# Late phase of a graph and mixture-of-experts kernel: 13 routing rounds with plans of their own, expert results added onto the output by DMA

## The chip, the cores and the metric

The kernel runs on 1 core of one Trainium2 chip. The metric is the device time of one execution in microseconds (us); lower is better. A core has a matrix engine (TensorE, PE in the profile), a vector engine (VectorE, DVE), a scalar engine (ScalarE, ACT), GpSimd (POOL) and SyncE (SP). The engines run their own programs in order and wait for each other by semaphores. SP, ACT and POOL issue DMAs; POOL issues the indirect ones, whose row numbers lie in a tile.

## The reference

Data is float32. 12,500 nodes with 256 features pass through a graph attention layer and a mixer block, whose sum with the input is x. The last layer, the one that this change is about, is a mixture of 8 experts in which each node uses its best two:

```
x = x + gnn(xn) + mix(xn)
xf = layernorm(x)
logits = xf @ gate_w + gate_b                   # 8 experts
probs = softmax(logits)
top2_vals, top2_idx = top_k(probs, 2)
cw = zeros(N, 8).at[arange(N)[:, None], top2_idx].add(top2_vals)
for each expert e:
    h = gelu(xf @ W1[e] + b1[e])                # 256 -> 512
    y = h @ W2[e] + b2[e]                       # 512 -> 256
    acc = acc + cw[:, e] * y
out = x + acc
```

## The kernel before

Four stages with barriers between them make the graph layer and the mixer; they end about 2,500 us into the program and the change does not touch them. After the last barrier comes the late phase, which has three kinds of work. A tile of nodes is 128 nodes (98 of them); a super is 4 node tiles (25 of them).

**Routing** takes a super from `xm_d` (mixer result) and `frag` (graph result, gathered by POOL into `e_fr`), adds them (`e_x`), stores the sum to `x1_d`, normalises it (`e_hn`, on DVE), transposes it on PE, multiplies by the gate and finds, in a chain of small DVE operations over a pair of supers, each node's two experts, their weights and its rows in a list for each expert. POOL then scatters each node's normalised features twice into `sorted_d`, once for each expert. The nodes are cut in two `PARTS` (56 and 42 node tiles). Only when a part is routed in full does `plan_vector` work out which expert tile holds which rows.

**Expert tiles** have 256 rows of one expert: 63 in the first part and 49 in the second, 112 in all, because each expert's last tile of a part is padded. W1 and W2 of all experts lie in SBUF. For each tile j there is `start` (PE turns the tile over, ACT copies it, DVE copies the expert's W1 to `w1c` and works out where results go and with what weight), `first` (16 matmuls with W1, ACT applies gelu), `second` (16 matmuls with W2) and `store` (DVE adds the bias and multiplies by the weight; POOL scatters the rows to `result_d`). `fetch` is SP's load of the tile into `gin`.

**Combining** reads the two results of each node and x1, adds them on DVE and stores `out`, super by super.

The order on every engine is written by generators that yield at the same steps: `back_half` routes part 0 alone, then runs the 63 tiles of part 0 with the routing of part 1 between them, three route steps at each yield, then the 49 tiles of part 1 with the combining of part 0 between them, then combines part 1. Within this, `tile_order` puts the pieces in this order on every engine: first(j), start(j+1), fetch(j+2), second(j-1), store(j-1). The fetch of before waits for these alone:

```
        if j >= 2:
            sp.wait_ge(S.x_tp, j - 1)
            sp.wait_ge(S.x_aim, j - 1)
```

`x_tp` counts tiles turned over on PE, `x_aim` tiles whose destinations DVE has worked out, `x_f1` halves of fc1 done, `x_h` gelus, `x_f2` tiles whose second is done, and `x_st` the two DVE operations of `store` (2 for each tile).

## Time and profile before

| | |
|---|---|
| time, median of 3 runs | 3830.7 us (3829.39 to 3833.43) |
| the profiled execution's own time | 3831.84 us |
| its span, first to last instruction | 3830.6 us |
| mean granted clock of TensorE | 0.863 of full speed |
| late phase | 2,500 us to the end |

The span is what the instructions cover; the profiled execution took 1.24 us more than that. The late phase is 1,331 us of it, and only there do the two kernels differ. Times in the rows further on are counted from the start of the span.

### The profile page before, as it was taken

The page shows a single profiled execution, that of the slowest core. Times are in us where ns is not written, and L with a number is a line of the kernel's source. Part 1 is how long each engine was busy: PE and PEld are TensorE (multiplying, and loading weights), DVE is VectorE, ACT ScalarE, POOL GpSimd, SP SyncE. Part 2 cuts the span into 40 slices and gives each one's busy share as a digit, 9 for nine tenths or more (in the row PEclk, how much of TensorE's full clock was granted, in tenths as well). Part 3 has the DMA queues.
Part 4 walks back from the last instruction along what each step waited for, and adds up shares of the span by engine and source line. Part 5 has one row for each costly group of instructions (what it writes and reads, how often), then busy time and mean ns, then how long its engine had stood idle before and what let it go on. Part 6 is the DMA issues. An engine that isn't in the chain of part 4 may idle for free.

```text
span 3830.6 us, 43808 instructions
## 1 busy us (share of the span) xinstructions
PE 2905.6 (76%) x12222; PEld 2286.9 (60%) x12222; DVE 2282.7 (60%) x6122; ACT 1380.5 (36%) x3103; POOL 2203.9 (58%) x2244
## 2 busy tenths in 40 slices
PE   6966878877777778887777764545398899989990
PEld 5844655555555555565555553345387778878880
DVE  6526666667666676666766665567565655445542
ACT  2313545444544444544544543100022222222220
POOL 0047777777777777777777776157535534323330
PEclk9977989898899998998999987555588889999995
DMA  8865665566555665656555655176433323255427
GB/s 210 275 185 153 182 162 158 160 169 169 162 159 155 165 176 157 163 163 179 157 162 162 166 148 131 50 243 197 145 115 120 111 82 117 73 177 182 149 70 235
DMA packets 412379, 602.91 MB, mean 157 GB/s; under 512 B 64458, under 2 KB 323694, under 8 KB 411935
## 3 DMA queue, kind: packets, MB, share of 16 engines
q0 software_dynamic: 106608, 306.41, 27.8%
q1 hardware_dynamic: 232563, 220.56, 19.0%
q10 hardware_dynamic: 72892, 72.50, 7.6%
q8 instruction: 104, 1.70, 0.2%
q14 instruction: 212, 1.74, 0.1%
HBM read 400.40 MB, written 198.88 MB: 156 GB/s over the span
## 4 chain that ended last, share of the span: by engine, by line
PE 51%; DMA 13%; POOL 12%; DVE 11%; issue 7%; ACT 4%; SPq 1%; ACTq 0%; DVEq 0%; POOLq 0%
PE bank L953 14%; PE bank L1732 9%; PE bank L1720 8%; DMA rows<-table,srcix 6%; PE bank L808 6%; POOL sorted_d L1330 5%; POOL rows L890 4%; PE bank L800 4%; DMA m_xs<-in_x 3%; DVE rows L1086 2%; PE bank L520 2%; DMA out<-c_x 2%; PE bank L512 1%; PE bank L513 1%; POOL e_fr L1313 1%
## 5 line engine op out<-in xcount | busy, mean ns | idle before, releaser
L890 POOL DMA_INDIRECT rows<-table,srcix x1664 | 1609.2, 967 | 506.9 <-issue 364.6
L953 PE MATMUL bank<-rows,onehot 128*128 128x272 f32 x3328 | 937.3, 431 | 30.4 <-ACT fout L1003 26.2
L1003 ACT ACTIVATE fout<-bank 128x272 f32<-128x272 f32 x1664 | 640.6, 398 | 480.5 <-PE bank L953 431.7
L953 PEld LDWEIGHTS bank<-rows,onehot 128*128 128x128 f32 x3328 | 675.0, 211 | 223.4 <-ACT fout L1003 46.6
L1086 DVE TENSOR_TENSOR rows<-rows,bank 128x1024 f32<-128x1024 f32 x416 | 482.7, 1213 | 183.3 <-ACT rows L994 183.3
L1808 POOL DMA_INDIRECT result_d<-x_y,x_dest x224 | 256.6, 1145 | 571.8 <-DVE x_y L1799 532.5
L1732 PE MATMUL bank<-e_w,x_ht 128*128 x1792 | 430.3, 396 | 7.1 <-DVE x_y L1795 6.3
L1720 PE MATMUL bank<-x_int,x_w1c 128*128 128x256 f32 x1792 | 416.3, 386 | 4.8 <-ACT x_int L1744 2.6
L1752 ACT ACTIVATE x_ht<-bank,x_b1c 128x256 f32<-128x256 f32 x448 | 187.1, 470 | 602.2 <-PE bank L1720 602.2
L1732 PEld LDWEIGHTS bank<-e_w,x_ht 128*128 128x128 f32 x1792 | 349.3, 200 | 56.5 <-issue 8.8
L1720 PEld LDWEIGHTS bank<-x_int,x_w1c 128*128 128x128 f32 x1792 | 346.7, 194 | 54.6 <-ACT x_int L1744 3.5
L935 PE MATMUL bank<-ident,sc_e 128*128 128x128 f32 x104 | 39.5, 379 | 331.7 <-ACT sc_e L983 331.7
L800 PE MATMUL bank<-m_hnt,fc_w 128*128 128x512 f32 (+1 forms) x600 | 287.0, 602 | 0.0
L1795 DVE TENSOR_TENSOR x_y<-bank,x_b 128x512 f32<-128x512 f32 x112 | 77.4, 691 | 317.2 <-PE bank L1732 310.4
L808 PE MATMUL bank<-fc_w,m_hid 128*128 128x256 f32 x1176 | 263.5, 381 | 0.0
L935 PEld LDWEIGHTS bank<-ident,sc_e 128*128 128x128 f32 x104 | 16.4, 157 | 382.6 <-ACT sc_e L983 367.2
L808 PEld LDWEIGHTS bank<-fc_w,m_hid 128*128 128x128 f32 x1176 | 225.0, 191 | 32.5
L1330 POOL DMA_INDIRECT sorted_d<-e_hn,e_row x196 | 197.7, 1009 | 73.7 <-issue 58.2
L1053 DVE TENSOR_TENSOR onehot<-bank,loc 128x2048 f32<-128x2048 f32 x104 | 237.4, 2282 | 0.0
L983 ACT ACTIVATE sc_e<-rows 128x256 f32<-128x256 f32 x104 | 43.3, 416 | 409.5 <-DMA rows<-table,srcix 399.5
L1059 DVE SCALAR_TENSOR_TENSOR g_sdm<-notself,bank 128x128 f32<-128x128 f32 x104 | 29.9, 288 | 265.7 <-PE bank L936 264.2
L800 PEld LDWEIGHTS bank<-m_hnt,fc_w 128*128 128x128 f32 x600 | 121.1, 202 | 89.9 <-issue 74.8
(336 smaller groups left out, 3645.4 us busy)
## 6 DMA issues: line engine op xcount, KB each, us to landing
frag<-fout ACTq DMA_DIRECT2D x104, 544.0 KB
x_in<-sorted_d SPq DMA_DIRECT2D x112, 260.0 KB, 2.9
rows<-table,srcix POOLq DMA_INDIRECT x1664
c_y<-result_d SPq DMA_DIRECT2D x48, 512.0 KB, 4.7
frag<-zero SPq DMA_DIRECT2D x7, 1904.0 KB, 9.1
table<-hr SPq DMA_DIRECT2D x24, 544.0 KB, 4.5
xs<-in_x SPq DMA_DIRECT2D x24, 512.0 KB, 8.0
xnt_d<-xt SPq DMA_DIRECT2D x24, 512.0 KB, 7.6
```

Of the source, the lines that this page charges most:

```text
L800: t = pe.matmul(bank[BANK_H[m % 2]][:, 0:n * P], B.mw1[:, kk, m * P:(m + 1) * P], B.m_hnt[:, kk, 0:n * P], start=(kk == 0), stop=(kk == KD ...
L808: t = pe.matmul(bank[BANK_Y[i // 2]][:, j * D:(j + 1) * D], B.m_hid[:, m, (i + j) * P:(i + j + 1) * P], B.mw2[:, m, :], start=(m == 0), st ...
L890: p.indirect_dma_start(out=B.rows[b][:, j, :], out_offset=None, in_=B.table[:, :], in_offset=bass.IndirectOffsetOnAxis(ap=B.srcix[:, col:c ...
L953: pe.matmul(B.banks[2 + c % 3][:, 0:ROW], B.onehot[k % 2][:, j, :], B.rows[k % NR][:, j, :], start=True, stop=True).then_inc(S.sum, 1)
L1003: a.activation(B.fout[k % 2][:, j, :], B.banks[2 + c % 3][:, 0:ROW], ACT.Copy).then_inc(S.ev, 1)
L1053: v.tensor_tensor(B.onehot[b][:, :, :], B.banks[0][:, 2 * P:3 * P].unsqueeze(1).to_broadcast([P, CB, P]), B.loc[:, k * CB:(k + 1) * CB].un ...
L1086: v.tensor_tensor(h, h, w.unsqueeze(3).to_broadcast([P, n, GH, GF]), ALU.mult).then_inc(S.wgh, 1)
L1330: p.indirect_dma_start(out=B.sorted_d[:, :], out_offset=bass.IndirectOffsetOnAxis(ap=B.e_row[:, j, s + i:s + i + 1], axis=0), in_=B.e_hn[k ...
L1720: t = pe.matmul(out, B.w1c[u][:, k, m * P:(m + 1) * P], B.gt[u][:, k, :], start=(k == 0), stop=(k == KD - 1))
L1732: t = pe.matmul(bk[BANK_OUT][:, i * D:(i + 1) * D], B.ht[u][:, m, i * P:(i + 1) * P], B.w2[:, bass.ds(ex * HT + m, 1), :], start=(m == 0), ...
L1752: a.activation(B.ht[u][:, m, :], B.banks[BANKS_H[m * 2 // HT]][:, m % 2 * ET:(m % 2 + 1) * ET], ACT.Gelu, bias=B.b1c[u][:, m:m + 1]).then_ ...
L1808: p.indirect_dma_start(out=B.result_d[:, :], out_offset=bass.IndirectOffsetOnAxis(ap=B.dest[j % (NOUT + 1)][:, i:i + 1], axis=0), in_=B.y[ ...
```

## The change

The nodes are routed in 13 rounds of two supers (the last has one, of two node tiles). A round works on 8 node tiles in one piece: DVE does the statistics of all 8 together, ACT instead of DVE writes the normalised features, and after the round's small operations `plan_vector` plans at once those expert tiles that are already full. A table fixed at build time says how many tiles each round plans: 0, 9, then 8 in each of ten rounds, and 16 in the last, which also takes the padded ones: 105 in all. A second loop, `late`, runs 4 route steps at each yield of `tile_order`, and there are four yields for a tile now. Tile 0 starts when two rounds are routed.

x goes straight to `out`, from ACT's queue. The scatter of a tile's results is an indirect DMA with addition onto `out`; each waits until the previous tile's has landed. `result_d`, `x1_d` and the combining are gone. W1 is no longer kept in SBUF: for each tile, SP loads the expert's W1 (512 KB), b1 and b2 (broadcast, 128 KB) into one of `NW` = 3 buffers ahead of the tile's rows. DVE's copy of W1 is gone, and its eight small operations for destinations and weights are three. The gate's bias is added on DVE and not by a matmul.

```diff
-NF, NH, W = 3, 4, 2 * ST
+NF, NH, NW, W = 2, 3, 3, 2 * ST
...
-ROUTE_STEPS = 3
+ROUTE_STEPS = 4
...
+ROUNDS = [list(range(k, min(k + 2, NS))) for k in range(0, NS, 2)]
...
 def experts_sync(sp, S, B):
     def fetch(j):
-        p, i = TILE_OF[j]
-        sp.wait_ge(S.planned, p + 1)
-        sp.wait_ge(S.e_z[p], 16 * (EXPERTS + 1))
-        for k in list(PARTS[p]["supers"])[-NH:]:
-            sp.wait_ge(S.e_g[k % NH], sent_to(k))
+        r, u, w = ROUND_OF[j], j % 2, j % NW
+        sp.wait_ge(S.planned, planned_by(j))
+        at = sp.value_load(B.tile_row[0:1, j:j + 1], min_val=0, max_val=ZERO_ROWS)
+        ex = sp.value_load(B.expert[0:1, j:j + 1], min_val=0, max_val=EXPERTS - 1)
+
+        if j >= NW:
+            sp.wait_ge(S.x_f1, 2 * (j - NW + 1))
+            sp.wait_ge(S.x_h, HT * (j - NW + 1))
+            sp.wait_ge(S.x_st, 2 * (j - NW + 1))
+        sp.wait_ge(S.x_w, 16 * (EXPERTS + 1))
+        sp.dma_start(B.w1c[w][:, :, :], B.a["L0_ffn_W1"].rearrange("e (k p) n -> p e k n", p=P)[:, bass.ds(ex, 1), :, :]).then_inc(S.x_wc[w], 16)
+        sp.dma_start(B.b1c[w][:, :], B.b1[:, bass.ds(ex, 1), :]).then_inc(S.x_wc[w], 16)
+        sp.dma_start(B.b2c[w][:, :], B.a["L0_ffn_b2"][bass.ds(ex, 1), :].to_broadcast([P, D])).then_inc(S.x_wc[w], 16)
+        sp.wait_ge(S.e_z, 16 * (EXPERTS + 1) if r == len(ROUNDS) - 1 else 16)
+        for q in range(max(r - NH + 1, 0), r + 1):
+            sp.wait_ge(S.e_g[q % NH], sent_to(q))
         if j >= 2:
             sp.wait_ge(S.x_tp, j - 1)
             sp.wait_ge(S.x_aim, j - 1)
...
 def experts_pool(p, S, B):
     def store(j):
+
+        r = ROUND_OF[j]
         p.wait_ge(S.x_st, 2 * j + 2)
+        for q in range(max(r - NF + 1, 0), r + 1):
+            p.wait_ge(S.e_x1[q % NF], stored_to(q))
+        if j:
+            p.wait_ge(S.x_y[(j - 1) % NOUT], 32 * ((j - 1) // NOUT + 1))
         for i in range(SUB):
-            p.indirect_dma_start(out=B.result_d[:, :],
-                                 out_offset=bass.IndirectOffsetOnAxis(ap=B.dest[j % (NOUT + 1)][:, i:i + 1], axis=0),
-                                 in_=B.y[j % NOUT][:, i, :], in_offset=None).then_inc(S.x_y[j % NOUT], 16)
...
+            p.indirect_dma_start(out=B.out[:, :], out_offset=bass.IndirectOffsetOnAxis(ap=B.dest[j % (NOUT + 1)][:, i:i + 1], axis=0),
+                                 in_=B.y[j % NOUT][:, i, :], in_offset=None, bounds_check=N_NODES - 1, oob_is_err=False,
+                                 compute_op=ALU.add).then_inc(S.x_y[j % NOUT], 16)
...
+def late(route, tiles):
+
+    rounds = 0
+    for needed in tiles:
         for _ in range(ROUTE_STEPS):
-            next(route, None)
+            rounds += next(route, None) is True
+        while rounds <= needed:
+            rounds += next(route) is True
+    for _ in route:
         pass
```

On SP's queue, this stood in a row for two tiles of part 1 before (`r_tile_row` is the planned row of the tile; e_x is a load for routing):

```order
L1364 DMA e_x<-xm_d 128x4x256 [waits e_hn_ready,e_x1_out1]
L1694 TENSOR_LOAD r_tile_row [waits e_sorted_out0,e_sorted_out1,e_sorted_out3,x_turned,e_sorted_out2,x_aimed,e_pad_out0,planned]
L1694 ISA x2
L1695 ISA
L1695 DMA x_in<-sorted_d 128x2x260
```

and now, for one late tile (the semaphore `x_y_read_scaled` is `x_st`, `x_turned` is `x_tp`, `x_gelu_done` is `x_h`, `x_fc1_done` is `x_f1`):

```order
L1664 TENSOR_LOAD pl_tile_row [waits planned]
L1664 ISA x2
L1665 TENSOR_LOAD pl_expert
L1665 ISA x2
L1672 ISA [waits x_y_read_scaled,x_weights_in,x_gelu_done,x_fc1_done]
L1672 DMA x_w1c<-in_L_ffn_W 128x2x512
L1673 ISA
L1673 DMA x_b1c<-x_b 128x4
L1674 ISA
L1674 DMA x_b2c<-in_L_ffn_b 128x256
L1681 ISA [waits e_sorted_out1,x_turned,e_sorted_out0,x_aimed,e_sorted_out2,e_pad_out]
L1681 DMA x_in<-sorted_d 128x2x260
```

The tile's own load, `x_in`, stands behind three other DMAs and behind a wait for `x_y_read_scaled` that was not there.

On PE, the order around a tile is the same in both; of the changed kernel, from the end of one second to the start of the next:

```order
L1719 MATMUL bank<-e_w,x_ht 128x256 x5
L1706 MATMUL bank<-x_int,x_w1c 128x256 [waits x_gelu_done,x_wc_in2,x_in_copied]
L1706 MATMUL bank<-x_int,x_w1c 128x256 x7
L1695 MATMUL bank<-ident,x_in 128x128 [waits x_in_copied,x_in1]
L1695 MATMUL bank<-ident,x_in 128x128 x3
L1713 TENSOR_LOAD pl_expert [waits planned]
L1713 ISA x2
L1719 ISA [waits x_y_read_scaled,x_weights_in,x_gelu_done]
L1719 MATMUL bank<-e_w,x_ht 128x256
```

The turn-over of a tile (`x_in`) stands between one tile's first and another's second, so a second waits behind it when `x_in` is not there. What is new is only the weights' semaphore `x_wc_in2`.

On POOL, in the stretch with the first tiles, there stands now:

```order
L1787 DMA out<-x_y,x_dest 12500x256 [waits e_x1_out1,x_out0,e_x1_out0,x_y_read_scaled]
L1787 DMA out<-x_y,x_dest 12500x256
L1300 DMA sorted_d<-e_hn,e_row 102656x260 [waits e_rows_ready]
L1300 DMA sorted_d<-e_hn,e_row 102656x260 x3
L1787 DMA out<-x_y,x_dest 12500x256 [waits e_x1_out1,x_out1,e_x1_out0,x_y_read_scaled]
L1787 DMA out<-x_y,x_dest 12500x256
L1300 DMA sorted_d<-e_hn,e_row 102656x260 x12
L1286 DMA e_fr<-frag,nodeix 128x272 [waits e_x1_ready]
L1286 DMA e_fr<-frag,nodeix 128x272 x7
```

Between two stores of tiles there are up to 12 + 8 = 20 DMAs of the routing.

## Rows read from the trace of the kernel before

**Rows 1.** The page, busy time by engine, and TensorE's clock in 40 slices.

```profile
PE 2905.6 (76%) x12222; PEld 2286.9 (60%) x12222; DVE 2282.7 (60%) x6122; ACT 1380.5 (36%) x3103; POOL 2203.9 (58%) x2244
...
PEclk9977989898899998998999987555588889999995
```

**Rows 2.** Windows: length, engines' busy time, granted clock, DMA share, GB/s.

```profile
2500.00:2760.00 260.00, 118.25 (x476) 108.25 (x476) 174.09 (x777) 18.51 (x35) 179.28 (x180) 0.50 0.63 203
2760.00:3215.00 455.00, 413.38 (x1944) 360.63 (x1945) 267.16 (x1113) 126.70 (x264) 203.54 (x197) 0.90 0.34 107
3400.00:3736.00 336.00, 334.91 (x1639) 294.60 (x1637) 178.49 (x558) 96.89 (x224) 110.94 (x92) 1.00 0.44 141
3740.00:3830.00 90.00, 0.00 (x0) 0.00 (x0) 25.89 (x22) 0.00 (x0) 0.37 (x1) 0.50 0.77 245
```

**Rows 3.** Timeline of one tile of part 1: start, duration, engine, line.

```profile
3647.07 0.60 PE L1709 MATMUL bank<-ident,x_in 128*128 128x128 f32 x4
...
3647.51 3.62 PE L1732 MATMUL bank<-e_w,x_ht 128*128 x16
...
3650.96 3.62 PE L1720 MATMUL bank<-x_int,x_w1c 128*128 128x256 f32 x16
3651.27 0.69 DVE L1795 TENSOR_TENSOR x_y<-bank,x_b 128x512 f32<-128x512 f32 x1 [2.40 <-PE bank L1732]
3652.00 0.69 DVE L1799 TENSOR_TENSOR x_y<-x_y,x_scale 128x512 f32<-128x512 f32 x1
...
3652.97 1.42 POOL L1808 DMA_INDIRECT result_d<-x_y,x_dest  x1 [4.66 <-DVE x_y L1799]
...
3654.85 3.62 PE L1732 MATMUL bank<-e_w,x_ht 128*128 x16
```

**Rows 4.** The tile view of x_in: min, median, max in ns; first and last start.

```profile
L1709 PE MATMUL bank<-ident,x_in x448: 272/273/475, 2760.8 to 3720.9; 128*128 128x128 f32 x150
L1695 SPq DMA_DIRECT2D x_in<-sorted_d x112: 372/373/877, 2758.0 to 3707.3; - x112
...
DMA to landing us min/median/max: 2.6/2.9/7.8
```

**Rows 5.** The tile view of e_w: loads of 512 KB of expert weights.

```profile
L1349 SPq DMA_DIRECT2D e_w<-in_L_ffn_W x16: 469/508/517, 2500.9 to 2602.5; - x16
...
DMA to landing us min/median/max: 5.1/6.8/10.0
```

**Rows 6.** Timeline of PE after a wait for gathered rows, in the edge stage.

```profile
2305.86 0.47 PE L935 MATMUL bank<-ident,sc_e 128*128 128x128 f32 x1 [7.63 <-ACT sc_e L983]
...
2306.34 5.25 PE L953 MATMUL bank<-rows,onehot 128*128 128x272 f32 x16
...
2312.55 3.84 PE L953 MATMUL bank<-rows,onehot 128*128 128x272 f32 x16
```

**Rows 7.** Timeline of a second that stands behind gate matmuls of the routing.

```profile
2818.29 5.06 PE L1732 MATMUL bank<-e_w,x_ht 128*128 x16
```

**Rows 8.** Timeline of PE where part 1's tiles begin.

```profile
3361.19 0.60 PE L1709 MATMUL bank<-ident,x_in 128*128 128x128 f32 x4
```

**Rows 9.** Timeline of the routing of part 0, its first gather and first super.

```profile
2500.06 0.97 POOL L1313 DMA_INDIRECT e_fr<-frag,nodeix  x1 [0.18 <-issue]
...
2509.93 0.18 DVE L1464 TENSOR_SCALAR e_rs<-e_fr 128x32 f32<-128x32 f32 x1 [9.84 <-DMA e_fr<-frag,nodeix]
...
2518.86 1.94 PE L1401 MATMUL bank<-ident,e_hn 128*128 128x128 f32 x8 [29.02 <-DVE e_hn L213]
```

**Rows 10.** Timeline of the last pair of part 0: small operations of the routing.

```profile
2711.72 0.99 PE L1410 MATMUL bank<-e_gw,e_hnt 128*128 128x8 f32 x4 [0.73 <-issue]
...
2717.70 0.22 DVE L1494 COPY e_lg<-bank 128x64 f32<-128x64 f32 x1 [4.84 <-PE bank L1411]
...
2727.87 0.16 DVE L1564 COPY e_hn<-e_rank 128x4 f32<-128x4 f32 x1
...
2729.02 0.96 POOL L1330 DMA_INDIRECT sorted_d<-e_hn,e_row  x1 [0.30 <-issue]
```

More of the change, by code:

```diff
@@ L1256, in merge_vector, with back_steps, round_steps @@
             v.tensor_tensor(to, to, part, ALU.add).then_inc(S.mg_sum, 1)
[L1261 to L1290 removed]
+MOMENTS = 4 * 2
+FRONT = MOMENTS + MOMENT_STEPS + 4
+PLAN = 6
+def back_steps(n):
+    return 28 + 2 * n
+def round_steps(r):
+    return FRONT + back_steps(R_TILES[r]) + PLAN
 def route_pool(p, S, B):
@@ L1335, in route_pool @@
[L1335 to L1351 removed]
+    p.iota(B.num[:, :], pattern=[[1, MOST]], base=0, **whole).then_inc(S.e_const, 1)
@@ new lines, in route_pool, with fetch @@
+    p.iota(B.region[:, :], pattern=[[REGION, EXPERTS]], base=0, **whole).then_inc(S.e_const, 1)
+    def fetch(r):
+        if r >= NF:
+            p.wait_ge(S.e_rx1, 2 * (r - NF + 1))
+        for i in range(R_TILES[r]):
+            at = R_FIRST[r] + i
+            p.indirect_dma_start(out=B.e_fr[r % NF][:, i, :], out_offset=None, in_=B.frag[:, :],
+                                 in_offset=bass.IndirectOffsetOnAxis(ap=B.nodeix[:, at:at + 1], axis=0)).then_inc(S.e_f[r % NF], 16)
+    fetch(0)
@@ new lines, in route_pool @@
+    for r in range(len(ROUNDS)):
+        n = R_TILES[r]
+        if r + 1 < len(ROUNDS):
+            fetch(r + 1)
+        yield from idle(FRONT + 28)
+        yield from idle(n)
+        p.wait_ge(S.e_row, r + 1)
+        for i in range(n):
+            for j in range(2):
+                at = R_FIRST[r] + i
+                p.indirect_dma_start(out=B.sorted_d[:, :], out_offset=bass.IndirectOffsetOnAxis(ap=B.e_row[:, j, at:at + 1], axis=0),
+                                     in_=B.e_hn[r % NH][:, i, :], in_offset=None).then_inc(S.e_g[r % NH], 16)
+            yield
+        yield from idle(PLAN)
+        yield True
@@ new lines, with tile_order, call @@
+BANK_IN, BANKS_H, BANK_OUT = 4, (5, 6), 7
+def tile_order(first=None, start=None, second=None, store=None, fetch=None):
+    def call(step, j):
+        if step:
+            step(j)
+    for j in (0, 1):
+        yield ROUND_OF[j]
+        call(fetch, j)
+    call(start, 0)
+    for j in range(SLOTS + 1):
+        now = ROUND_OF[min(j + 1, SLOTS - 1)]
+        if j < SLOTS:
+            call(first, j)
+            yield now
+        if j + 1 < SLOTS:
+            call(start, j + 1)
+            yield now
+        if j + 2 < SLOTS:
+            yield ROUND_OF[j + 2]
+            call(fetch, j + 2)
+        if j:
+            call(second, j - 1)
+            yield now
+            call(store, j - 1)
@@ L1734, in second @@
         t.then_inc(S.x_f2, 1)
-    return tile_order(first, start, second, None)
+    return tile_order(first=first, start=start, second=second)
 def experts_scalar(a, S, B):
```

720 lines of the change are left out of this document (286 added, 434 removed).

## Prediction

> **What bounds the kernel now.** I read the page first. Over the whole program no engine is full [rows 1]; the clock row shows TensorE at full speed only near the end, and at half speed where the routing of part 0 stands. The change touches only what follows 2,500 us, so the next view is the windows [rows 2]. They divide the late phase into four stretches with four different limits:
>
> - 2,500 to 2,760: routing alone. PE works at half clock, 118 of 260 us; POOL and DVE are busy 179 and 174. This is a chain of small operations and gathers, for 56 node tiles, 37 us for 8 of them.
> - 2,761 [rows 4] to 3,361 [rows 8]: the 63 tiles of part 0 with 42 node tiles routed between them, 600.4 us.
> - 3,361 to 3,736: 49 tiles and the hidden half of the combining. PE is busy 334.9 of 336 us at clock 1.00 and is the bound.
> - 3,736 to the end: combining of part 1, DMA share 0.77, no matmul, 94 us.
>
> The timeline of one tile gives its price [rows 3]: second starts at 3647.51, the next one at 3654.85, so 7.34 us. Hence the routing between tiles costs before: 600.4 − 63 × 7.34 = 138 us for 42 node tiles, 26.3 us for 8.
>
> **What would be saved if nothing else moved.** The last stretch (94 us) goes. Seven tiles fewer are 7 × 7.34 = 51 us. Tile 0 waits for two rounds of 8 node tiles instead of 56. When does it start? The first gather is issued at 2500.1, and with 4 gathers DVE began at 2509.9 [rows 9]; each further gather adds 0.96 + 0.30 = 1.26 us on POOL (a scatter's row, same spacing [rows 10]), so with 8 it begins at 2515. From there to the first transposes one super took 2518.86 − 2509.93 = 8.9 us; two supers in one piece cost between once and twice that, since the wide operations double and the dozen small ones do not: I take 14. Then 32 transposes at 1.94 us for 8 (7.8), 16 gate matmuls at 0.99 us for 4 (4.0), 1 for the copies, and the small operations to the last tail column, 2727.87 − 2717.70 = 10.2 [rows 10]. One round is 37 us, and rounds no longer overlap each other, so two are 74: 2589. Then 16 scatters × 1.26 = 20 us, and some 3 + 3 us until they and the tile's own load have landed: tile 0 is on PE at 2616, against 2761. This saves 145 us. Up to here the change is worth 290 us, less whatever the larger share of routing beside the tiles (82 node tiles instead of 42) costs.
>
> **The new wait, which I think decides.** Look at the rows of SP's queue beside those of PE. fetch(j+2) now may not issue anything before `x_st` is at 2j, which means that store(j−1) is done on DVE, because W1's buffer and b2's are three deep and tile j−1 has the buffer that tile j+2 wants. And `x_in` of tile j+2 is the fourth DMA behind that wait, although its own two buffers were free long before. On PE the turn-over of tile j+2 stands right behind first(j+1), and second(j) behind it. So there is a closed chain from one second to the next, and its parts are in the rows:
>
> 1. from the start of second(j−1) to the end of L1799: 3652.69 − 3647.51 = 5.2 us [rows 3];
> 2. SP wakes and issues. POOL, released by the same operation, began 0.28 us after it. Then W1's issue, 0.51 [rows 5], b1's and b2's, 0.37 each [rows 4], and three gaps of some 0.2 for register instructions and waits: `x_in` is issued about 2.2 us after L1799;
> 3. its landing: 2.9 us in the median before, at least 2.6 [rows 4], but now with 640 KB ahead of it on the same queue. A load of 512 KB took 5.1 to 10.0, median 6.8 [rows 5]; if x_in arrived a microsecond behind such a W1 it would be there 0.3 + 6.8 + 1 = 8.1 us after L1799. Bounds for items 2 and 3 together are thus 4.9 and 8.1; I take 5.6, near the low end, since the queues carried 0.44 of the DMA time in the steady stretch [rows 2] and W1 starts 1.7 us before x_in;
> 4. from the turn-over's start to second: 3647.51 − 3647.07 = 0.44, and 0.06 for the release.
>
> Sum: 5.2 + 5.6 + 0.5 = 11.3 us for a tile, bounds 10.6 and 13.8. In it PE has first(j+1), 3.45 us, to do, and then stands idle for some 4 us in each tile. That is the second half of the argument.
>
> **The clock.** At full clock 16 matmuls of second take 3.62 us. After 7.6 us of waiting in the edge stage the first 16 of L953 took 5.25, the next 16, 6 us later, 3.84 [rows 6], so 1.4 us were lost. Behind a stretch with nothing but transposes and gate matmuls a second took 5.06 instead of 3.62, 1.4 too [rows 7]. The stretch with most waits, 2,500 to 2,760, stayed at 0.50 throughout, though PE was busy 118 of 260 us [rows 2]. With an idle stretch and a turn-over in every tile I expect the second behind it, which is on the chain, to pay this each time: between 0 (the clock holds) and 1.8 (all of it at half speed would be 3.45 more, half of it 1.7). I take 1.4: 12.7 us for a tile. The Trainium skill, "TensorE: Matmul & The Clock Gate", Part 1 ("What's actually happening"), says that the throttled state is the default and that activity releases it, and Part 4 that transposes do not count as activity in the same way. By that page the idle time and the turn-over in every tile would cost the clock in every tile; were it wrong here, the term would be nothing and the sum 147 us less, which is the first rival.
>
> **Routing beside the tiles.** If all of it were hidden in PE's 4 idle us, it would cost nothing; at the old rate it would cost 82/8 × 26.3 = 270 us. PE's own part for 8 node tiles at full clock is about 7 us against 4.75 tiles × 4 us of idleness (a round has 76 steps, a tile takes 16). But half of the steps stand between a turn-over and its second, and there a wait for ACT's normalised rows or DVE's chain lengthens the loop. I take a quarter of the old rate, 6.6 us for 8 node tiles: 67 us.
>
> **Things that I cost at nothing.** DVE loses the W1 copy and five small operations, 2 us a tile, in time in which it waited for PE (2.40 us idle ahead of L1795 [rows 3]). POOL issues a tile's store in 1.42 + 0.30 + 0.96 = 2.7 us [rows 3, 10] and must now wait for the previous one's landing; with 12.7 us a tile, that is covered as long as adding takes less than about 10 us to land. A burst of 20 routing DMAs (25 us) between two stores is two tiles long, and three buffers of `y` cover it. Moving x to `out` instead of `x1_d` changes no bytes. Behind the last second come 1.7 us to L1799, 2.7 of issue and about 3 of landing: 7 us.
>
> **Sum, in the profiled execution's time.** 2616 + 105 × 12.7 (1333.5) + 67 + 7 = 4023.5 span, + 1.2 outside it = 4024.7; the median of the runs lay 1.1 below the profiled one, so I say 4024 us, 5.0% slower.
>
> **Rivals.**
>
> - *Late loads at full clock.* As above, but the clock holds: 105 × 11.3 = 1186.5, so 3878. For it: the idle time is half that of rows 6. Against it: rows 7. 0.18.
> - *Faster: the loads are early enough.* This one ends on the other side. If `x_in` lands within 5.0 us of L1799 and the clock holds, a tile takes 10.6, and with the routing nearly hidden (20 us) the time is 2616 + 1113 + 20 + 7 + 1 = 3757. The point from which it decides: 3830.6 − 2616 − 67 − 7 = 1141.6 us for 105 tiles, 10.87 for one, clock losses included. The extreme is that the change does just what it says and PE stays the bound: 2616 + 771 + 270 + 8 = 3665; for that, fetch(j+2) would have to land inside first(j+1), which only the order above contradicts. Together 0.17.
> - *Slower still: W1 or the adding stores set the pace.* If loads of 512 KB take their 6.8 us and the clock goes too, a tile takes 5.2 + 8.1 + 0.5 = 13.8 and some clock. If a store with addition takes 11.5 us to land, POOL's issue and wait make 2.7 + 11.5 = 14.2 a tile. Either way some 14.2: 2616 + 1491 + 67 + 9 = 4183. No row shows a DMA that adds; plain ones landed in 2.9. 0.15.
> - The likeliest, late loads with clock losses: 0.50, by itself 3930 to 4110.
>
> A measurement of this kernel tells about 0.2% from no change. Faster by more than that 0.17, within it 0.03 (between the first and second rival), slower 0.80. The range of 3800 to 4185 leaves out most of the faster case and the tail of the slowest.
>
> **What the changed profile would show.** Steps right: late tiles (after about 60 of 105) at 11 to 14 us from second to second instead of 7.34; PE's wait for `x_in` on the turn-over near 4 us a tile and the costliest in the late phase; `x_in` issued some 2.2 us after the second operation of store; the clock of that stretch below 1.00, near 0.8. Tile 0 on PE near 2616. Wrong, if PE is again full at clock 1.00 in the last 50 tiles; if the wait ahead of PE is for `x_wc` (then W1 and not `x_in` is late) or DVE's is for stores to land (then the adding is); or if the stretch with routing runs more than 2 us a tile slower than that without, which would say that I made the routing too cheap.

## The result, and the profile after

The changed kernel takes 4331.3 us (median of 4 runs, 4323.4 to 4339.9) where the kernel before takes 3832.1 beside it (4 runs, 3829.4 to 3833.9). The ratio is 1.1304, its 95% interval 1.128 to 1.1328: 499 us slower. The prediction had 192 slower. The sign and the mechanism hold; the size does not, and 4331 lies outside the range of 3800 to 4185.

The page of the changed kernel, busy time and TensorE's clock in 40 slices, as [rows 1]:

```profile
PE 3035.7 (70%) x11774; PEld 2337.2 (54%) x11774; DVE 2011.6 (46%) x5108; ACT 1434.1 (33%) x3176; POOL 2274.2 (52%) x2227
...
PEclk9969999989989999889987557777777778787787
```

PE has 448 matmul records fewer and is busy 130 us longer. The clock row says why: from about 2,600 us to the end it mostly stands at 7 and 8, where before it was at 8 beside routing and at 9 in the tiles alone [rows 1]. The windows of the late phase (length, busy time of PE, PEld, DVE, ACT and POOL, granted clock, DMA share, GB/s), beside [rows 2]:

```profile
2650.00:3556.00 906.00, 610.18 (x2373) 505.23 (x2372) 310.84 (x1287) 203.44 (x403) 393.69 (x334) 0.77 0.47 126
3600.00:4200.00 600.00, 389.93 (x1420) 316.13 (x1418) 73.00 (x197) 90.35 (x199) 123.63 (x80) 0.80 0.33 78
```

The first row holds the first 52 tiles with routing beside them, the second is tiles alone. No engine is full in either. The clock of 0.77 and 0.80 is a mix of the two levels, 1.2 GHz (0.50) and 2.4 GHz (1.00): below, a tile's second of 16 matmuls takes 5.94 us behind PE's idle time, and the first of 16 that follows 3.62. In the second, DVE, ACT and POOL are busy an eighth, a seventh and a fifth of the time; something makes them all wait. The chain of waits says what: DMA x_in is 11% of the chain over the whole program. The waits after 2,620 us (engine, tile, line, what it waited for: total us, times, longest) agree:

```profile
POOL out L1787 <- DVE x_y L1772: 948.8, 78, 32.2
...
DVE x_dest L1756 <- DMA x_in<-sorted_d: 661.4, 99, 8.3
...
PE bank L1695 <- DMA x_in<-sorted_d: 529.3, 99, 8.7
```

The largest of them is harmless: POOL waits for work that does not exist yet. PE's 529.3 us on the turn-over of a tile is the loss. The timeline of one steady tile, from store to store, beside [rows 3]:

```profile
4103.12 0.69 DVE L1772 TENSOR_TENSOR x_y<-x_y,x_scale 128x512 f32<-128x512 f32 x1
4104.10 0.37 SPq L1672 DMA_DIRECT2D x_w1c<-in_L_ffn_W  x1
...
4104.63 0.50 SPq L1673 DMA_DIRECT2D x_b1c<-x_b  x1
4105.31 0.45 SPq L1674 DMA_DIRECT2D x_b2c<-in_L_ffn_b  x1
...
4106.12 0.37 SPq L1681 DMA_DIRECT2D x_in<-sorted_d  x1
4106.44 1.55 POOL L1787 DMA_INDIRECT out<-x_y,x_dest  x1 [0.30 <-issue]
...
4111.41 1.12 PE L1695 MATMUL bank<-ident,x_in 128*128 128x128 f32 x4 [5.60 <-DMA x_in<-sorted_d]
...
4112.32 5.94 PE L1719 MATMUL bank<-e_w,x_ht 128*128 x16
...
4118.10 3.62 PE L1706 MATMUL bank<-x_int,x_w1c 128*128 128x256 f32 x16
...
4119.02 0.69 DVE L1772 TENSOR_TENSOR x_y<-x_y,x_scale 128x512 f32<-128x512 f32 x1
```

Read it as a loop: store ends at 4103.81; 2.31 us later `x_in` is issued as the fourth DMA; 5.29 us later PE can turn it over; 0.91 us after that second begins; 7.39 us later the next store ends. That is 15.90 us for this tile; the 50 tiles whose L1772 starts between 3555.5 and 4314.3 took 15.18 each. The same four parts, as means over these tiles, worked out from the start of each x_in issue, turn-over, second and store in the trace of each kernel (e3 and e7 are told below):

| part of the loop | predicted | changed kernel | e7, no add | e3, x_in first |
|---|---|---|---|---|
| store's end to x_in's issue | 2.2 | 2.37 | 2.38 | 0.29 |
| issue to PE's turn-over | 3.4 | 4.88 | 4.19 | 2.77 |
| turn-over to second | 0.5 | 0.91 | 0.90 | 1.04 |
| second to the store's end | 5.2 + 1.4 clock | 7.03 | 6.49 | 5.27 |
| sum | 12.7 | 15.19 | 13.96 | 9.37 |

The loop is the predicted one. Of the 2.5 us that are over, 1.5 lie in the second row, the landing; the tile view of x_in gives it too (issue to landing; min, median, max), against 2.9 in [rows 4]:

```profile
L1681 SPq DMA_DIRECT2D x_in<-sorted_d x105: 372/373/384, 2612.8 to 4303.1; - x105
...
DMA to landing us min/median/max: 2.9/4.8/7.1
```

The third row is a matter of the clock. In the tile above the four turn-over matmuls start 0.21 to 0.27 us apart and second starts 0.21 us behind the last of them, with no idle time between; at full clock in [rows 3] they start 0.11 us apart. The wider spacing is there in 47 of the 48 steady tiles from 55 to 102.

### The profile page after: what moved, and what is told of

It reads as the page before. It is cut to its first block, busy times and chain, and to the rows that moved or that the text cites. A ratio compares the mean times of both kernels' runs of the same rounds, so it can differ in the third digit from the quotient of the medians.

```text
span 4332.7 us, 42225 instructions
## 1 busy us (share of the span) xinstructions
PE 3035.7 (70%) x11774; PEld 2337.2 (54%) x11774; DVE 2011.6 (46%) x5108; ACT 1434.1 (33%) x3176; POOL 2274.2 (52%) x2227
## 4 chain that ended last, share of the span: by engine, by line
PE 45%; DMA 20%; DVE 14%; issue 7%; POOL 6%; ACT 5%; SPq 4%; ACTq 0%; POOLq 0%; DVEq 0%
PE bank L949 12%; PE bank L1719 11%; DMA x_in<-sorted_d 11%; DMA rows<-table,srcix 5%; PE bank L804 5%; PE bank L796 3%; POOL rows L886 3%; DMA m_xs<-in_x 3%; PE bank L1695 2%; DVE rows L1082 2%; PE bank L1370 2%; DVE x_y L1772 2%; DVE x_y L1768 2%; PE bank L516 1%; SPq L1673 1%
## 5 line engine op out<-in xcount | busy, mean ns | idle before, releaser
L886 POOL DMA_INDIRECT rows<-table,srcix x1664 | 1610.0, 968 | 506.9 <-issue 355.8
L949 PE MATMUL bank<-rows,onehot 128*128 128x272 f32 x3328 | 942.7, 433 | 30.9 <-ACT fout L999 26.2
L1787 POOL DMA_INDIRECT out<-x_y,x_dest x210 | 328.4, 1564 | 1041.3 <-DVE x_y L1772 948.8
L949 PEld LDWEIGHTS bank<-rows,onehot 128*128 128x128 f32 x3328 | 679.1, 212 | 225.6 <-ACT fout L999 45.6
L1719 PE MATMUL bank<-e_w,x_ht 128*128 x1680 | 575.9, 517 | 1.8 <-DVE x_y L1768 1.0
L1082 DVE TENSOR_TENSOR rows<-rows,bank 128x1024 f32<-128x1024 f32 x416 | 483.1, 1215 | 179.4 <-ACT rows L990 179.4
L1719 PEld LDWEIGHTS bank<-e_w,x_ht 128*128 128x128 f32 x1680 | 446.1, 273 | 110.4 <-issue 13.6
L1695 PE MATMUL bank<-ident,x_in 128*128 128x128 f32 x420 | 114.2, 426 | 558.4 <-DMA x_in<-sorted_d 558.4
L1695 PEld LDWEIGHTS bank<-ident,x_in 128*128 128x128 f32 x420 | 73.8, 213 | 597.9 <-DMA x_in<-sorted_d 597.8
L1706 PE MATMUL bank<-x_int,x_w1c 128*128 128x256 f32 x1680 | 387.5, 384 | 1.4 <-ACT x_int L1731 1.4
L1706 PEld LDWEIGHTS bank<-x_int,x_w1c 128*128 128x128 f32 x1680 | 323.7, 193 | 47.0 <-ACT x_int L1731 2.0
L1756 DVE CAST x_dest<-x_in 128x2 int32<-128x2 f32 x105 | 18.9, 180 | 694.9 <-DMA x_in<-sorted_d 679.8
L1768 DVE TENSOR_TENSOR x_y<-bank,x_b2c 128x512 f32<-128x512 f32 x105 | 72.5, 691 | 432.5 <-PE bank L1719 432.5
L1731 ACT ACTIVATE x_int<-bank 128x512 f32<-128x512 f32 x105 | 62.7, 597 | 596.0 <-PE bank L1695 596.0
## 6 DMA issues: line engine op xcount, KB each, us to landing
x_b2c<-in_L_ffn_b SPq DMA_DIRECT2D x105, 128.0 KB, 4.8
```

What stands on the lines that cost most here:

```text
L886: p.indirect_dma_start(out=B.rows[b][:, j, :], out_offset=None, in_=B.table[:, :], in_offset=bass.IndirectOffsetOnAxis(ap=B.srcix[:, col:c ...
L949: pe.matmul(B.banks[2 + c % 3][:, 0:ROW], B.onehot[k % 2][:, j, :], B.rows[k % NR][:, j, :], start=True, stop=True).then_inc(S.sum, 1)
L1082: v.tensor_tensor(h, h, w.unsqueeze(3).to_broadcast([P, n, GH, GF]), ALU.mult).then_inc(S.wgh, 1)
L1695: t = pe.transpose(bk[BANK_IN][:, k * ET + i * P:k * ET + (i + 1) * P], B.gin[u][:, i, k * P:(k + 1) * P], B.ident[:, :])
L1706: t = pe.matmul(out, B.w1c[w][:, k, m * P:(m + 1) * P], B.gt[u][:, k, :], start=(k == 0), stop=(k == KD - 1))
L1719: t = pe.matmul(bk[BANK_OUT][:, i * D:(i + 1) * D], B.ht[u][:, m, i * P:(i + 1) * P], B.w2[:, bass.ds(ex * HT + m, 1), :], start=(m == 0), ...
```

## The experiments

Every kernel ran beside the kernel before on its own chip, and that matters here. On some chips the same program took longer than on others: the kernel before took 3830 to 3838 on the chips of the result, of c0 and c1 and of e5 to e8, and 4310 to 4336 on the three chips of the others. By e1 and e5, and by e6 and e14, which are the same kernels on either kind, the extra time lies in the stages ahead of the late phase and in routing; the tiles without routing take the same time on both (e6 and e14 below, 7.35 us). The changed kernel itself was timed on the faster chips only, so what an edit on a slower chip gained against it is an estimate by ratios. So whole times are compared as ratios to before on one chip, and mechanisms by steady tiles: "steady" is the mean over 50 tiles from the start of L1772 in tile 52 to that in tile 102, "beside routing" the mean over tiles 0 to 52. Routing's last scatter falls in tile 50 or 51 in all of them but e8 (tile 86, so its "steady" tiles have routing beside them) and e9 (tile 25).

| kernel | before, us | this, us | ratio | steady | beside routing |
|---|---|---|---|---|---|
| changed kernel | 3832 | 4331 | 1.130 | 15.18 | 17.38 |
| c0 changed kernel again | 3838 | 4319 | 1.125 | 14.80 | 17.40 |
| c1 kernel before again | 3838 | 3837 | 1.000 | - | - |
| e7 no add in the scatter | 3830 | 4242 | 1.107 | 13.96 | 16.92 |
| e5 rows first | 3830 | 3740 | 0.977 | 7.61 | 13.20 |
| e6 rows first, 4 buffers | 3830 | 3711 | 0.969 | 7.35 | 12.99 |
| e8 as e6, 2 route steps | 3830 | 3827 | 0.999 | 10.55 | 12.42 |
| e1 as e5 | 4336 | 4238 | 0.977 | 7.55 | 14.99 |
| e2 4 buffers | 4336 | 4227 | 0.975 | 7.36 | 14.64 |
| e3 order only | 4336 | 4373 | 1.009 | 9.37 | 16.04 |
| e4 PE filled | 4336 | 4854 | 1.120 | 14.26 | 20.10 |
| e9 as e6, 8 route steps | 4329 | 4214 | 0.973 | 7.35 | 14.85 |
| e10 as e6, NOUT 6 | 4329 | 4175 | 0.964 | 7.35 | 14.17 |
| e11 as e10 | 4310 | 4158 | 0.964 | 7.35 | 14.25 |
| e12 as e3 | 4310 | 4340 | 1.007 | 9.53 | 15.49 |
| e13 as e2 | 4310 | 4147 | 0.962 | 7.36 | 14.12 |
| e14 as e6 | 4310 | 4182 | 0.971 | 7.35 | 14.30 |

Intervals of the ratios: e1 0.9771 (0.974 to 0.9802), e2 0.9749 (0.9719 to 0.9779), e5 0.9766 (0.975 to 0.9783), e6 0.9689 (0.9673 to 0.9705), e8 0.9987 (0.9976 to 0.9998), e9 0.9726 (0.967 to 0.9782), e10 0.9636 (0.9579 to 0.9693), e11 0.9635 (0.9596 to 0.9673), e12 1.0072 (1.0046 to 1.0098), e14 0.9711 (0.9683 to 0.9739). c0, c1, e3, e4 and e7 ran once. e13's row is its profiled run; its other one took 4217 us, a ratio of 0.979. The changed kernel and c0 differ in nothing but a comment line, and their steady tiles by 0.38 us: differences of that size between single traces mean little.

### e1: the rows' load ahead of the store's wait

```diff
     def fetch(j):
...
+        (the waits for e_z, e_g, x_tp, x_aim and the x_in load stand here)
         if j >= NW:
             sp.wait_ge(S.x_f1, 2 * (j - NW + 1))
             sp.wait_ge(S.x_h, HT * (j - NW + 1))
             sp.wait_ge(S.x_st, 2 * (j - NW + 1))
```

> The changed kernel, with one edit on SyncE: a tile's rows (x_in) are issued ahead of the wait for W1's buffer instead of behind it and behind the three weight loads. Late-load theory: in the changed kernel a late tile takes 15.2 us because x_in leaves only after the store of tile j-1; now it leaves a tile earlier, so late tiles fall to 7.3 to 8.5 us, the clock of that stretch goes to 1.00, and the time to 3560 to 3720 us. Rival, the weights: W1 still leaves after that store; if it is not there for first(j+2), PE waits for it instead and a tile stays at 10 to 11 us, some 3950 us. Rival, the adding stores: if they set the pace, late tiles stay above 13 us and the time above 4100 us.

Measured: 4238, ratio 0.9771 (0.974 to 0.9802) to the kernel before on that chip, steady tiles 7.55 us instead of 15.18, and the clock from 3,850 to 4,200 us at 1.00. The tile is as the late-load theory has it. The time by its ratio, 0.9771 × 3832 = 3744 us, is over that theory's 3560 to 3720; the tiles beside routing, of which the expectation did not speak, kept 15.0 us. Taking `x_in` out of the loop takes the idle time and the clock loss away together.

### e2: a fourth weight buffer

```diff
-NF, NH, NW, W = 2, 3, 3, 2 * ST
+NF, NH, NW, W = 2, 3, 4, 2 * ST
```

> The changed kernel with NW = 4 buffers for W1, b1 and b2 instead of 3, the order of the loads unchanged. Late-load theory: fetch(j+2) then waits for the store of tile j-2, which is long done, so x_in is in time although three weight loads stand ahead of it: late tiles 7.3 to 8.5 us and the time within 60 us of the kernel that issues the rows first. If it is the queue's order and not the wait that makes x_in late, this changes less than 100 us from 4331. Adding stores as the pace: no change.

Measured: 4227, ratio 0.9749 (0.9719 to 0.9779), steady tiles 7.36 us. It is 11 us from e1 on the same chip, within the 60 allowed. Here the order of the four loads is untouched; only the store that fetch waits for is one tile older.

### e3: the order of the loads alone

```diff
             sp.wait_ge(S.x_st, 2 * (j - NW + 1))
+        (the waits for e_z, e_g, x_tp, x_aim and the x_in load stand here)
         sp.wait_ge(S.x_w, 16 * (EXPERTS + 1))
         sp.dma_start(B.w1c[w]...)
```

> The changed kernel, the wait for W1's buffer kept where it was, but x_in issued ahead of W1, b1 and b2. This prices the place in the queue by itself: x_in would be issued 0.5 us after the second operation of store instead of 2.3 and land in 2.9 instead of about 5, so a late tile takes 15.2 - 1.8 - 2.2 = 11.2 us, somewhat less if the clock recovers, and the time is some 3900 us (3800 to 3980). Were the landing slow for another reason (the adding stores on the same 16 engines), only 1.8 us a tile go and it is 4140.

Measured: 4373, steady tiles 9.37 us. All waits are kept, the loop stays closed, and yet 5.8 of the 15.2 us go. The timeline of one of its tiles:

```profile
3999.66 0.38 SPq L1677 DMA_DIRECT2D x_in<-sorted_d  x1
...
4002.27 0.66 PE L1695 MATMUL bank<-ident,x_in 128*128 128x128 f32 x4 [0.90 <-DMA x_in<-sorted_d]
...
4003.17 3.71 PE L1719 MATMUL bank<-e_w,x_ht 128*128 x16 [0.24 <-issue]
...
4007.65 0.69 DVE L1772 TENSOR_TENSOR x_y<-x_y,x_scale 128x512 f32<-128x512 f32 x1
4008.62 0.37 SPq L1677 DMA_DIRECT2D x_in<-sorted_d  x1
```

From the store's end at 4008.34 to the issue 0.28 us instead of 2.31; from the issue at 3999.66 to PE's turn-over 2.61 instead of 5.29; turn-over to second 0.90, as in the changed kernel; from second to the store's end 5.17 instead of 7.39. The last is the clock: at 0.99 in this stretch, against 0.80. The expectation of 11.2 us for a tile had kept the clock loss, and 9.37 is below it by 1.8, as much as the clock gave back; the time by its ratio, 1.0086 × 3832 = 3865 us, lies within 3800 to 3980. The 0.90 to second is here made otherwise than in the changed kernel: the turn-over's matmuls run at full clock, and PE then stands idle for 0.24 us in this tile, 0.4 in the mean, for a reason that the trace does not show. The window with the clock:

```profile
4000.00:4200.00 200.00, 169.55 (x774) 138.58 (x773) 41.05 (x108) 49.85 (x110) 68.05 (x44) 0.99 0.56 130
```

### e4: PE filled with matmuls

```diff
+        for m in range(FILL):    # FILL = 16
+            pe.matmul(bk[BANK_IN][:, 0:ET], B.w1c[w][:, m % KD, 0:P], B.gt[u][:, m % KD, :], start=True, stop=True)
```

These stand behind first(j) and their results are overwritten.

> The changed kernel with 16 matmuls that serve nothing (into the bank of the next turn-over, overwritten by it) on PE between first(j) and start(j+1), where it waits for x_in. They fill 3.5 of some 5.6 us of waiting. If the half clock of the second behind the wait costs what its rows show (16 matmuls in 4.8 to 5.8 us instead of 3.45, the turn-over 0.9 instead of 0.44), a late tile falls from 15.2 to about 13.2 us and the time by some 200 us, to 4130. If the clock is not what costs there, the time stays within 20 us of 4331 or rises.

Measured: 4854, steady tiles 14.26 us. The fill came out as 32 records and 7.07 us, so PE itself was the bound, and the kernel's time, far above the 4130 us expected, says nothing about a gain. What it does show is in the window and four rows:

```profile
4500.00:4700.00 200.00, 200.00 (x956) 176.09 (x955) 26.18 (x71) 31.88 (x70) 43.29 (x28) 1.00 0.34 81
```

```profile
4502.90 0.37 SPq L1682 DMA_DIRECT2D x_in<-sorted_d  x1
...
4507.94 0.17 DVE L1759 CAST x_dest<-x_in 128x2 int32<-128x2 f32 x1 [7.37 <-DMA x_in<-sorted_d]
...
4509.31 0.60 PE L1696 MATMUL bank<-ident,x_in 128*128 128x128 f32 x4
4509.74 3.62 PE L1722 MATMUL bank<-e_w,x_ht 128*128 x16
```

At clock 1.00 the turn-over takes 0.60 and the second 3.62 us, against 1.12 and 5.94 in the changed kernel. The load, 5.04 us from issue to use on DVE, is as late as it was: its lateness does not come from the clock. And the turn-over does not cost the clock by itself: here, as in e6, every tile has one.

### c0 and c1: both kernels unedited

```diff
+# the kernel as it is
```

> Nothing is edited but one comment line. All four kernels so far begin their late phase some 400 us later than the changed kernel, though their instructions ahead of it are word for word the same. Theory A (the edits in the late phase move something that the earlier stages feel): this one gives 4335 us as the changed kernel does, with the first tile at about 2616 us. Theory B (the instructions are not the cause; where a program lies in memory, or how the time was taken, is): it may come out near 4740 us, with the first tile near 3020 us, and all four kernels then have to be compared with this one in place of the changed kernel.

> The kernel before with one comment line added. Theory A: 3832 us. Theory B: some 400 us more, near 4240 us, the extra time all in the stages ahead of the late phase, which would show that the disturbance has nothing to do with the change.

Measured: 4319 and 3837, as expected by theory A. That the four kernels above began their late phase 400 us late was therefore neither building nor edits, and the time that stood beside them as that of the kernel before, 4336, tells the rest: it went with the chip on which they ran. My expectation for c0 had taken that 4336 for the changed kernel's.

### e5: e1's kernel on an ordinary chip

> The kernel of e1 again, the x_in load ahead of the waits for the store and ahead of the three weight loads, on a chip where the kernel before takes its usual 3832 us. In e1's trace the stages ahead of the late phase ran about 410 us longer than in the unedited kernel's, and the kernel before took 4335 us beside it. Theory A (that chip was slower for every kernel in those stages, and e1's edit is innocent of it): first store near 2652 us, tiles without routing beside them at 7.4 us, 52 tiles at about 15 and 52 at 7.4, so 3820 us, between 3770 and 3840: level with the kernel before or a little faster. Theory B (the edit slows the earlier stages): about 4237 us again, with the first store near 3060 us.

Measured: 3740, first store at 2651.35, so theory A; the time is below its span of 3770 to 3840, since the tiles beside routing took 13.2 us here and 15.0 on e1's chip.

### e6: rows first and four buffers

> Both cures at once, the x_in load first and NW=4 weight buffers. If the wait for the store is all that stretched the tiles, nothing is left for the second cure: steady tiles 7.3 us and the time within 15 us of e5. If routing beside the tiles also feels the lead that the loads have, the first 52 tiles shorten and it is up to 60 us faster than e5.

Measured: 3711, 29 us under e5, steady tiles 7.35 against 7.61. Twice the 15 us that the first theory allowed, but most of it, 13 us, is in the steady tiles, which with three buffers still waited now and then, and 11 us beside routing.

### e7: the scatter without its add

```diff
-                                 in_=B.y[j % NOUT][:, i, :], in_offset=None, bounds_check=N_NODES - 1, oob_is_err=False,
-                                 compute_op=ALU.add).then_inc(S.x_y[j % NOUT], 16)
+                                 in_=B.y[j % NOUT][:, i, :], in_offset=None, bounds_check=N_NODES - 1, oob_is_err=False).then_inc(S.x_y[j % NOUT], 16)
```

> The changed kernel with the add taken out of its output scatter (the routed nodes' rows then lack what was in the output before: that part is left out), everything else as it was, the wait for the store too. Theory 1 (the x_in rows land late, 5.3 us against the 3.4 that I took, because the adding scatter of the tile before is moving at the same time): landing falls to about 3.5 us, tiles from 15.2 to 13.3 us, 4331 to about 4150 us. Theory 2 (they land late because 640 KB of W1, b1 and b2 stand ahead of them on the same queue, as e3 makes likely): tiles stay at 15 us and only the issue of the scatter shrinks, so 4300 to 4335 us.

Measured: 4242, steady tiles 13.96. Between the two theories. One tile of it, and its view of x_in:

```profile
4113.77 0.37 SPq L1681 DMA_DIRECT2D x_in<-sorted_d  x1
4117.74 1.07 PE L1695 MATMUL bank<-ident,x_in 128*128 128x128 f32 x4 [4.29 <-DMA x_in<-sorted_d]
...
4118.61 5.01 PE L1719 MATMUL bank<-e_w,x_ht 128*128 x16
```

```profile
DMA to landing us min/median/max: 2.9/4.2/7.1
```

Over the steady tiles, issue to turn-over is 4.19 us against 4.88 in the changed kernel and 4.64 in c0, the same kernel again; e3, with the load in front, has 2.77. So 0.4 to 0.7 of the 1.9 to 2.1 us comes from the add in the scatter that moves at the same time, and 1.4 is there without it. The shorter idle time also gives back 0.4 to 0.5 us of clock. A tile gains 1.2 us against the changed kernel and 0.8 against c0, not the 1.9 of theory 1.

The 1.4 us are not taken apart further. In e3 `x_in` goes out ahead of all three loads, but also 0.5 us ahead of the tile's scatter, where in the changed kernel it goes out 1.5 us behind the scatter's start. The landings say one thing more. In the steady tiles of the changed kernel W1 (512 KB) has landed 1.3 us after `x_in` is issued, b2 (128 KB) 4.2 us after it and `x_in` itself 4.8 us after it. Of the loads ahead, only b2's is still moving for most of that time. The view of DMAs (KB, median us from issue to landing, from 3,800 to 4,200 us):

```profile
x_w1c<-in_L_ffn_W SPq DMA_DIRECT2D x27, 512.0 KB, 3.3
...
x_b2c<-in_L_ffn_b SPq DMA_DIRECT2D x27, 128.0 KB, 4.9
```

### e8 and e9: two and eight route steps

```diff
-ROUTE_STEPS = 4
+ROUTE_STEPS = 2      # e8;  8 in e9
```

> e6 with ROUTE_STEPS 2 in place of 4: fewer routing steps run ahead of each tile. If routing's own chain sets the first 52 tiles (it has to finish a round before the tiles that need it), spreading it thinner over more tiles hides more of it, and it is 20 to 80 us faster than e6. If each engine's queue only stalls at other places, it is within 20 us of e6; slower if the rounds come late and tiles wait for them.

> e6 with ROUTE_STEPS 8 in place of 4. e8 (2 steps) cost 116 us against e6, and its tiles showed a gap of 30 us once in every round of eight tiles, where DVE and PE wait for x_in: the rounds come late. Theory A (routing is best got ahead early): 8 steps take the gaps away altogether and the time falls by another 10 to 60 us from 3711. Theory B (with 4 steps the gaps already come from POOL's line, 16 sorted_d scatters at 1.26 us each behind and ahead of out scatters that wait for the landing of the one before): the work per round is the same and so is the time, within 20 us of 3711; more if DVE's and PE's tile work is held behind routing.

Measured: e8 3827, 116 us over e6 on the same chip. Each round now comes late for its tiles: routing lasts to about tile 87, and the wait view between 2,650 and 3,430 shows PE waiting for x_in again, up to 20.9 us at a time, since the rows of its round are not yet scattered into `sorted_d` (the last case that the expectation named):

```profile
PE bank L1695 <- DMA x_in<-sorted_d: 185.3, 15, 20.9
```

e9 stands at 0.973 and e14, the same with 4 steps on another chip of that kind, at 0.971: no difference that these runs can tell, which is theory B's. Routing ends by tile 25 instead of 51, but each of those tiles then pays more.

### e10 and e11: six output buffers, against e14

```diff
-NOUT = 3
+NOUT = 6
```

> e6 with NOUT 6 in place of 3: twice as many y, dest and scale buffers. In e6 DVE waits 151 us between 2650 and 3330 for the landing of an older tile's out scatter ahead of x_dest (25 times, 17.8 us the longest), and routing's own DVE work is queued behind that wait. Theory A (that wait is what holds the routing up): most of the 151 us goes, and the time falls by 60 to 150 us from 3711. Theory B (POOL's own line of scatters is full, and DVE's wait only shows it): the wait moves on to another instruction and the time stays within 20 us of 3711.

> The kernel of e10 again (both cures and NOUT 6) beside e14, the kernel of e6 again, since e10 ran on a chip where the kernel before took 4329 us and e6 on one where it took 3830. Against its own kernel before, e10 stood at -154 us and e6 at -119 us. Theory A (the wait of x_dest for the landing of an older scatter did hold up routing): 20 to 60 us faster than e14 on any chip, so about 3675 us where before takes 3830. Theory B (the difference was the chip's): within 10 us of e14.

> The kernel of e6 again, as the measure for e11 on the same chip: ratio to before 0.969 as then, 3711 us where before takes 3830.

What led to it are the waits of e6 between 2,650 and 3,330 us:

```profile
DVE x_dest L1756 <- DMA out<-x_y,x_dest: 150.7, 25, 17.8
PEld bank L1360 <- ACT e_hn L1405: 133.6, 16, 24.6
PE bank L1360 <- ACT e_hn L1405: 124.7, 10, 24.3
ACT e_hn L1405 <- DVE e_st L1465: 111.9, 10, 21.3
```

DVE waits in order for an old scatter; the routing's statistics are queued behind it, ACT's rows behind those, PE's transposes behind these. Measured: e10 4175, ratio 0.9636 on its chip; by itself that could not tell its two theories apart, since e6 had run on another kind of chip. e11 4158, e14 4182 on one chip, 23 us apart (runs of 4137 to 4180 against 4174 to 4196). Between 3,050 and 3,750 us the wait of x_dest is 78.9 us in e14 (first fence) and gone from e11's view; but DVE's wait for the gate matmuls is 128.0 us in e14 and 199.6 in e11 (second fence):

```profile
DVE e_lg L1476 <- PE bank L1370: 128.0, 9, 18.9
...
DVE x_dest L1756 <- DMA out<-x_y,x_dest: 78.9, 13, 14.0
```

```profile
DVE e_lg L1476 <- PE bank L1370: 199.6, 9, 32.3
```

By the medians, theory A of e11 holds at the low end of its 20 to 60 us. The two traces cannot show the 23 us, since these two runs took the same time, 4180 and 4181 us; what they show is theory B of e10, the wait moving to the next one of the same in-order queues.

### e12 and e13: order only and buffers only, beside e14

> The kernel of e3 again: every wait of the changed kernel kept, only the x_in load issued ahead of W1, b1 and b2. With e3's own tiles (16.0 us beside routing there, less what that chip added, and 9.2 us without) it should stand near 3850 to 3880 us where before takes 3830. If the order of four transfers really is most of the 499 us, that is 450 us or more below the changed kernel.

> The kernel of e2 again: the order of the loads kept as in the changed kernel, only a fourth weight buffer, so that the fetch waits for a store one tile older. Theory A (the closed chain through the store is the whole loss): 3715 to 3740 us where before takes 3830, tiles of 7.3 us though x_in still lands 5 us after its issue. Theory B (landing behind the weights counts by itself): tiles over 8 us.

Measured: e12 4340, 1.0072 times before (1.0046 to 1.0098), as expected; against the changed kernel's 1.130 that is some 470 us by ratios. e13 4147 in its profiled run and 4217 in the other, too far apart to rank it against e14's 4182, but its tiles can be read. A tile of e13:

```profile
3954.14 3.62 PE L1719 MATMUL bank<-e_w,x_ht 128*128 x16
3954.22 0.38 SPq L1681 DMA_DIRECT2D x_in<-sorted_d  x1
...
3957.60 3.62 PE L1706 MATMUL bank<-x_int,x_w1c 128*128 128x256 f32 x16
...
3961.05 0.60 PE L1695 MATMUL bank<-ident,x_in 128*128 128x128 f32 x4
3961.49 3.62 PE L1719 MATMUL bank<-e_w,x_ht 128*128 x16
```

`x_in` is still issued 2.35 us after a store's end (3951.87) and still behind three loads, but nobody waits: the tile that it belongs to is a tile further away, and PE goes from second to first to turn-over without a gap, 7.35 us. So theory A holds in its tiles: an `x_in` that is issued behind the store and behind three loads costs only because the loop is closed through the store.

## Why the prediction was right in kind and wrong in size

- **Tile 0 at 2616: right.** PE's first turn-over in the changed kernel starts at 2615.73. The price of a round, worked out from [rows 9, 10] as 37 us, held (the same operation of rounds 0 and 1 is 36.6 us apart, 2543.98 and 2580.57), and with it the 145 us saved. It is not luck: the parts came out too, 14.5 us from DVE's start to the first transpose for the 14 taken.
- **The closed loop through `x_st`: right, and shown from both sides.** e2 and e13 undo it by one buffer, e1 and e5 by one move, and each of them takes the steady tile to 7.4 to 7.6 us.
- **Item 1, second's start to the store's end, 5.2: right** at full clock (5.17 in e3).
- **Item 2, issue of x_in 2.2 after the store: nearly right** (2.31 in the tile shown, 2.37 in the mean).
- **Item 3, the landing: this is the step that failed.** I had bounds of 4.9 and 8.1 for items 2 and 3 together and took 5.6, near the low end, because the queues carried 0.44 of the DMA time. Measured are 2.37 + 4.88 = 7.25, near the other end; the landing alone is 4.88 where I took 3.4, 1.5 us a tile. The share of busy time is a mean over a long stretch. In the changed kernel it is even lower, 0.33, while four loads start within 2.1 us of each other. The 640 KB ahead on the same queue stood in my own sentence and I priced them at half a microsecond. e3 shows the same load there for PE after 2.77 us when it goes first; e7 shows that the add is the smaller part. Which of the three loads ahead costs how much is open: the row that I feared, 6.8 us for a load of 512 KB, did not come back (W1 landed in 3.3), and b2's broadcast of 128 KB took 4.9.
- **Item 4, turn-over to second, 0.5: too small by 0.4.** It is 0.91, and this is the clock again, at a place where the sum had none: the four matmuls of the turn-over run at half clock and take twice as long. e3's 1.04 has another make, full clock and an idle gap, and its cause was not tried.
- **The clock, 1.4: right in kind, too small.** Second's start to the store's end took 7.03 in the mean against 5.17 at full clock, 1.86, some 0.4 more than the 1.4; with the 0.4 of the turn-over the clock cost 2.3 us a tile, over the upper bound of 1.8. By the Trainium skill, "TensorE: Matmul & The Clock Gate", Part 1, activity is what releases the throttle; e4, where PE was never idle, ran at 1.00, which agrees. e3 had a closed loop too, with PE idle for 1.1 us ahead of each turn-over and 0.4 behind it, and paid almost nothing (0.99); the changed kernel is idle for 5.2 us ahead of each turn-over. The lost clock belongs to that idle time, not to the loop. Nor does it belong to the turn-over, which the prediction had charged beside the idle time: e6 has the same turn-over in every tile and stood at 1.00 from 3,400 to 3,650 us.
- **Routing beside the tiles, 67: too cheap.** The changed kernel paid 17.38 − 15.18 = 2.2 us in each of 52 tiles, 114 us. The prediction had named more than 2 us as the sign of this. Its other signs came too: the clock of the steady stretch near 0.8 (0.80), `x_in` issued some 2.2 us after the store, PE waiting for `x_in` and not for W1.
- **Sum.** 105 tiles × 2.5 us = 262, and 47 for routing: 309, where 4331 − 4024 = 307 were missing. So 85% of the miss is the tile: 105 × 1.48 = 155 us for the landing, 88 for the clock (43 of it in the turn-over) and 18 for the issue. With the landing alone put right, the sum would have been 4179 us.
- **The rivals.** "Slower still" had the nearest price for a tile, 14.2, for W1 or for the adding store; the measured 15.2 is above even that. It named a loss of clock beside its 13.8 as "some" and gave it only 0.4 us. Neither of its two forms is what happened: PE waits for `x_in`, not for W1, and the landing of stores shows in PE's waits nowhere. The point at which faster turns to slower is 3830.6 − 2690 = 1140.6 us for 105 tiles, not 1141.6, which changes nothing. The extreme of the faster rival, 3665, is what e6 came near: 3711 when the loop is opened, with routing at 5.6 us in each of 52 tiles (293 us) where the rival took the old rate, 270.

A version that beats both kernels comes out of this. e6 is 3.1% faster than the kernel before (interval 3.0 to 3.3); e11, with deeper output buffers, 3.6% (3.3 to 4.0), though it was timed on the slower chips only.

## What to carry to other kernels

When a load is put behind a wait, draw the loop that it closes and price the last transfer issued behind the wait, with everything that the same queue was given in the same burst ahead of it; a low mean DMA share is no ground to take the low bound. Put the load that the matrix engine needs first at the head of the burst and its waits apart from those of buffers that are not needed yet: one moved block was worth about 470 us here (1.130 to 1.007), and one more buffer about 590 (1.130 to 0.975), both estimates by ratios from different chips. Idle gaps of PE of some 5 us were paid twice here, once as waiting and once as clock, and gaps of some 1 us only once, so a loop that is a little shorter can be a great deal faster.

## What the hardware showed unasked

**A scatter that adds.** POOL is busy 1.54 us with each instead of 0.97 (e7), and with the add the scatter's own landing took 5.3 us in the median instead of 4.3. In the kernel before, the plain scatter of a tile's results landed in 2.9 us; there no weights were loaded beside it.

**Slower chips.** The same kernel, e1 and e5, took 4238 and 3740 us. Of the 500 us, 410 lie ahead of the late phase. The two wait views from 500 to 2,500 us, first e1's and then e5's:

```profile
ACT fout L999 <- remote: 314.9, 145, 11.2
...
PEld bank L949 <- issue: 230.1, 211, 5.4
```

```profile
ACT fout L999 <- PE bank L949: 387.2, 388, 5.3
...
ACT sc_e L979 <- DMA rows<-table,srcix: 348.9, 75, 10.6
```

These names need care. The trace of e1 holds 26,009 semaphore events and that of e5 62,242, and the other traces from the slower chips are as short of them. "Remote" and "issue" may thus be waits whose release was not recorded, and they can't be read as the cause. What stands without them is that the engines are idle for longer over the same work. From the first to the last matmul of L949, with the same 6,126 matmul records on PE, e1 took 2453 us and e5 2097, and the idle time was 705 and 484 us on PE, 1091 and 741 on DVE. The single instructions take nearly what they took: one of L1082 on DVE 1.21 us in the mean in both, one of L886 on POOL 0.96 and 0.97, one of L949 on PE 0.45 and 0.43. The kernel before took 480 to 505 us more there in all; no trace of it from such a chip was kept. The steady expert tiles are not slower at all. No run here tells the cause, nor whether it belongs to the chips for good, since none was tried at two times. For a reader the lesson is plain: compare with the same kernel on the same chip, and never a trace of one with a trace of the other.
